# Self-attention of a PixArt block on one NeuronCore: another written order of a middle unit's steps

## The reference, cut to what matters

```python
def adaln(x, t, w, b):
    emb = t @ w + b
    scale, shift = jnp.split(emb, 2, axis=-1)
    return layernorm(x) * (1.0 + scale) + shift

def mha(xq, ctx, wq, wk, wv, wo, bo):
    q = (xq @ wq).reshape(b, sq, H, DH).transpose(0, 2, 1, 3)
    k = (ctx @ wk).reshape(b, sk, H, DH).transpose(0, 2, 1, 3)
    v = (ctx @ wv).reshape(b, sk, H, DH).transpose(0, 2, 1, 3)
    scores = jnp.einsum('bhqd,bhkd->bhqk', q, k) / math.sqrt(DH)
    attn = jax.nn.softmax(scores, axis=-1)
    out = jnp.einsum('bhqk,bhkd->bhqd', attn, v)
    return out.transpose(0, 2, 1, 3).reshape(b, sq, INNER) @ wo + bo

h1 = adaln(x, t, norm1_w, norm1_b)
x = mha(h1, h1, ...) + x          # self-attention, 1024 queries, 1024 keys
h2 = adaln(x, t, norm2_w, norm2_b)
x = mha(h2, context, ...) + x     # cross-attention, 77 keys
x = glu_ff(adaln(x, ...)) + x     # then a quantised feed-forward net
```

## Time and profile before

| | us |
|---|---|
| median of 3 runs | 1274.09 |
| lowest and highest run | 1270.73, 1281.41 |
| the profiled execution's own time | 1271.72 |
| its span in the trace | 1269.9 |
| PE busy in the span | 1130.8 |
| units 0 to 15 of self-attention, about | 61 to 815 |

### The profile page before, as it was taken

One profiled execution on the slowest core, in us unless ns is written; L12 is line 12 of the kernel. 1 busy time (PEld: TensorE's weight loads), 2 busy tenths in 40 slices (PEclk: granted clock), 3 DMA queues, 4 the chain that ended last, 5 costly groups with the idle time before them and its releaser, 6 DMA issues.

```text
span 1269.9 us, 30602 instructions
## 1 busy us (share of the span) xinstructions
PE 1130.8 (89%) x12732; PEld 736.7 (58%) x12739; DVE 867.5 (68%) x1724; ACT 593.1 (47%) x855; POOL 681.1 (54%) x602
## 2 busy tenths in 40 slices
PE   4789999999999999999999998988999799799776
PEld 1245655665665665655665665666666566365554
DVE  5667767756756667757757658578679666765764
ACT  3335454444344344444444455444445442465555
POOL 5657866755655666757755654356346443511230
PEclk7799999999999999999999999999999999999987
DMA  7230220220220220220220222234333520000001
GB/s 270 58 109 2 51 51 2 52 51 7 46 51 9 45 51 3 51 51 2 52 51 2 51 51 68 43 67 121 82 64 74 162 76 1 1 5 14 17 1 34
DMA packets 41855, 63.52 MB, mean 50 GB/s; under 512 B 11460, under 2 KB 22384, under 8 KB 41462
## 3 DMA queue, kind: packets, MB, share of 16 engines
q1 hardware_dynamic: 40413, 60.91, 19.1%
q10 hardware_dynamic: 1304, 0.66, 0.2%
HBM read 20.63 MB, written 2.10 MB: 18 GB/s over the span
## 4 chain that ended last, share of the span: by engine, by line
PE 61%; DVE 17%; DMA 7%; ACT 6%; issue 6%; SPq 2%; POOL 1%; ACTq 0%; DVEq 0%
PE outs L806 9%; PE scores L865 7%; PE scores L866 7%; PE mixed L827 6%; DMA head_operands<-neg_max_rows 5%; PE outs L783 4%; PE scores L924 4%; PE outs L890 3%; PE outs L888 3%; PE outs L889 3%; PE outs L940 3%; DVE maxes L1670 3%; DVE exps_rest L1693 2%; PE outs L816 2%; SPq L673 2%
## 5 line engine op out<-in xcount | busy, mean ns | idle before, releaser
L1459 POOL TENSOR_TENSOR exps_rest<-exps 128x1024 f16<-128x1024 f32 (+1 forms) x297 | 511.5, 1730 | 317.3 <-ACT exps L1169 316.5
L1169 ACT ACTIVATE exps<-scores 128x1024 f32<-128x1024 f32 (+1 forms) x320 | 296.8, 936 | 281.3 <-PE scores L866 251.7
L1670 DVE TENSOR_REDUCE maxes<-mixed 128x1 f32<-128x512 f32 x512 | 334.3, 684 | 81.1 <-PE mixed L827 77.6
L865 PE MATMUL scores<-head_operands 128*128 128x512 f16 (+1 forms) x576 | 219.8, 382 | 24.3 <-DMA head_operands<-neg_max_rows 23.7
L888 PE MATMUL outs<-values,exps 128*128 128x65 f16 (+1 forms) x2176 | 226.6, 193 | 1.2 <-POOL exps_rest L1459 1.2
L889 PE MATMUL outs<-values,exps 128*128 128x64 f16 (+1 forms) x2176 | 226.6, 192 | 0.0
L890 PE MATMUL outs<-values,exps_rest 128*128 128x65 f16 (+1 forms) x2176 | 226.4, 194 | 0.0
L866 PE MATMUL scores<-head_operands 128*128 128x512 f16 (+1 forms) x576 | 219.6, 381 | 0.0
L889 PEld LDWEIGHTS outs<-values,exps 128*128 128x128 bf16 (+1 forms) x2176 | 200.5, 98 | 24.8 <-issue 0.2
L888 PEld LDWEIGHTS outs<-values,exps 128*128 128x128 bf16 (+1 forms) x2176 | 201.6, 98 | 22.7 <-POOL exps_rest L1459 2.2
L890 PEld LDWEIGHTS outs<-values,exps_rest 128*128 128x128 f16 (+1 forms) x2176 | 200.4, 97 | 0.0
(11 more groups left out here) (200 smaller groups left out, 1599.7 us busy)
## 6 DMA issues: line engine op xcount, KB each, us to landing
head_operands<-qk_pairs SPq DMA_DIRECT2D x128, 256.0 KB, 4.2
head_operands<-qk_pairs SPq DMA_DIRECT2D x32, 128.0 KB, 2.4
stage<-in_L_xcond_ff_w_dram SPq DMA_DIRECT2D x3, 1024.0 KB, 5.6
residual<-in_x_dram SPq DMA_DIRECT2D x4, 512.0 KB, 9.7
stage<-in_L_ffn_w_dram SPq DMA_DIRECT2D x2, 1024.0 KB, 5.1
head_operands<-in_x_dram SPq DMA_DIRECT2D x1, 2048.0 KB, 10.2
out_dram<-out_tile SPq DMA_DIRECT2D x16, 128.0 KB, 1.7
attn_outT<-in_L_xcond_attn_wq_dram SPq DMA_DIRECT2D x1, 1024.0 KB, 8.2
```

Source lines behind the costliest of these rows:

```text
L865: mm(o, kb[:, KH, :], hb[:, QS, :], start=True, stop=False)
L1169: A(E[0:a.ks, c % RING, 0:n], SP_[c % 2][0:a.ks, 0:n], ACT.Exp, scale=SCALE).then_inc(s.exps, 1)
L1459: G.tensor_tensor(R[0:a.ks, c % RING, 0:n], e, e.bitcast(BF16).rearrange("p (n two) -> p n two", two=2)[:, :, 1], ALU.subtract).then_inc(s ...
L1670: V.tensor_reduce(mx[:, h, t, kh:kh + 1], m[:, :], AX_X, ALU.max).then_inc(s.maxed, 1)
```

## The change

Only the table `SELF_UNIT` and the lags change; no step is added or taken away. The old and the new order up to chunk 8, with the untouched steps left out:

```diff
 SELF_UNIT = (
-    ("scores", 1), ("rest", 0), ("max", 0, 1, 8), ("max", 0, 1, 9), ("q", 1, 0),
+    ("max", 0, 1, 8), ("scores", 1), ("rest", 0), ("max", 0, 1, 9), ("q", 1, 0),
...
-    ("slot", 1), ("slot", 2), ("slot", 3), ("values", 1), ("k", 1, 0), ("max", 0, 1, 12), ("scores", 4),
-    ("rest", 3), ("max", 0, 1, 13), ("k", 1, 1), ("values", 2), ("scores", 5), ("scores", 6), ("rest", 4),
-    ("rest", 5), ("max", 0, 1, 14), ("norm1", 0), ("max", 0, 1, 15), ("projB", 0), ("scores", 7), ("rest", 6),
-    ("values", 3), ("row", 0, 1), ("v", 1, 0), ("slot", 4), ("slot", 5), ("values", 4), ("values", 5),
-    ("max", 1, 0, 0), ("max", 1, 0, 1), ("normT1", 0), ("slot", 6), ("values", 6), ("scores", 8), ("rest", 7),
+    ("slot", 1), ("slot", 2), ("values", 1), ("k", 1, 0), ("scores", 4), ("scores", 5), ("k", 1, 1),
+    ("max", 0, 1, 12), ("rest", 3), ("max", 0, 1, 13), ("values", 2), ("rest", 4), ("rest", 5), ("scores", 6),
+    ("max", 0, 1, 14), ("norm1", 0), ("slot", 3), ("max", 0, 1, 15), ("projB", 0), ("rest", 6), ("values", 3),
+    ("row", 0, 1), ("rest", 7), ("v", 1, 0), ("slot", 4), ("scores", 7), ("slot", 5), ("values", 4),
+    ("normT1", 0), ("values", 5), ("max", 1, 0, 0), ("max", 1, 0, 1), ("values", 6), ("scores", 8),
...
-    ("scores", 12), ("slot", 10), ("rest", 11), ("max", 1, 0, 12), ("projA", 1), ("max", 1, 0, 13),
+    ("scores", 12), ("rest", 11), ("max", 1, 0, 12), ("max", 1, 0, 13),
+    ("slot", 10), ("projA", 1), ("lo1", 1), ("values", 10), ("norm", 1), ("max", 1, 0, 14), ("rest", 12),
...
-SELF_LAGS = {"POOL": {"proj": 5, "norm": -2},
-             "ACT": {"scores": -1, "row": 1},
-             "DVE": {"rest": -4}}
+SELF_LAGS = {"POOL": {"proj": 5, "norm1": 2, "lo": 1},
+             "ACT": {"scores": -1, "row": 1, "hi": 2, "q": -2},
+             "DVE": {"rest": -3, "v": -1, "k": 2}}
```

More of the change, by code:

```diff
@@ L63 @@
-    ("values", 3), ("row", 0, 1), ("v", 1, 0), ("slot", 4), ("slot", 5), ("values", 4), ("values", 5),
-    ("max", 1, 0, 0), ("max", 1, 0, 1), ("normT1", 0), ("slot", 6), ("values", 6), ("scores", 8), ("rest", 7),
-    ("max", 1, 0, 2), ("norm", 0), ("hi1", 0), ("max", 1, 0, 3), ("v", 1, 1), ("scores", 9), ("rest", 8),
-    ("max", 1, 0, 4), ("max", 1, 0, 5), ("values", 7), ("projA", 0), ("normT", 0), ("slot", 7),
-    ("max", 1, 0, 6), ("slot", 8), ("lo1", 0), ("norm1", 1), ("hi", 0), ("scores", 10), ("max", 1, 0, 7),
@@ L68 @@
-    ("values", 8), ("rest", 9), ("lo", 0), ("max", 1, 0, 8), ("scores", 11), ("rest", 10), ("max", 1, 0, 9),
-    ("hi1", 1), ("max", 1, 0, 10), ("projB", 1), ("slot", 9), ("values", 9), ("normT1", 1), ("max", 1, 0, 11),
-    ("scores", 12), ("slot", 10), ("rest", 11), ("max", 1, 0, 12), ("projA", 1), ("max", 1, 0, 13),
-    ("slot", 11), ("lo1", 1), ("values", 10), ("norm", 1), ("max", 1, 0, 14), ("rest", 12), ("values", 11),
-    ("normT", 1), ("scores", 13), ("hi", 1), ("slot", 12), ("max", 1, 0, 15), ("scores", 14), ("slot", 13),
@@ L73 @@
[L73 to L79 removed]
+    ("max", 0, 1, 8), ("scores", 1), ("rest", 0), ("max", 0, 1, 9), ("q", 1, 0), ("max", 0, 1, 10), ("slot", 0),
@@ new lines @@
+    ("normT1", 0), ("values", 5), ("max", 1, 0, 0), ("max", 1, 0, 1), ("values", 6), ("scores", 8),
+    ("max", 1, 0, 2), ("norm", 0), ("hi1", 0), ("slot", 6), ("max", 1, 0, 3), ("v", 1, 1), ("scores", 9),
+    ("rest", 8), ("max", 1, 0, 4), ("max", 1, 0, 5), ("values", 7), ("normT", 0), ("slot", 7), ("projA", 0),
+    ("max", 1, 0, 6), ("lo1", 0), ("slot", 8), ("rest", 9), ("norm1", 1), ("hi", 0), ("scores", 10),
+    ("max", 1, 0, 7), ("values", 8), ("rest", 10), ("lo", 0), ("max", 1, 0, 8), ("scores", 11),
@@ new lines @@
+    ("max", 1, 0, 9), ("hi1", 1), ("max", 1, 0, 10), ("projB", 1), ("slot", 9), ("values", 9),
+    ("max", 1, 0, 11), ("normT1", 1), ("scores", 12), ("rest", 11), ("max", 1, 0, 12), ("max", 1, 0, 13),
+    ("slot", 10), ("projA", 1), ("lo1", 1), ("values", 10), ("norm", 1), ("max", 1, 0, 14), ("rest", 12),
+    ("values", 11), ("normT", 1), ("hi", 1), ("slot", 11), ("slot", 12), ("scores", 13), ("max", 1, 0, 15),
+    ("scores", 14), ("slot", 13), ("rest", 13), ("max", 1, 1, 0), ("row", 1, 0), ("values", 12),
@@ new lines @@
+    ("max", 1, 1, 1), ("lo", 1), ("rest", 14), ("scores", 15), ("values", 13), ("rest", 15), ("max", 1, 1, 2),
+    ("max", 1, 1, 3), ("slot", 14), ("out", 0, 0), ("scores", 16), ("max", 1, 1, 4), ("values", 14),
+    ("max", 1, 1, 5), ("values", 15), ("max", 1, 1, 6), ("max", 1, 1, 7), ("slot", 15), ("out", 0, 1),
+    ("slot", 16))
+SELF_LAGS = {"POOL": {"proj": 5, "norm1": 2, "lo": 1},
+             "ACT": {"scores": -1, "row": 1, "hi": 2, "q": -2},
+             "DVE": {"rest": -3, "v": -1, "k": 2}}
```

7 lines of the change are left out of this document (1 added, 6 removed).

## The result

| | before | after |
|---|---|---|
| median of 4 runs each, same chip, us | 1272.76 | 1257.78 |
| lowest and highest | 1270.73, 1281.41 | 1256.14, 1259.88 |
| profiled execution: time, span | 1271.72, 1269.9 | 1259.88, 1258.1 |

The ratio of the runs, after to before, is 0.9866, with a 95% interval of 0.984 to 0.9891: faster by 1.3%, just over the 1% that a measurement of this kernel can tell. (The two medians alone give 0.988.) The forecast for the median was 1258.5. The profiled execution is the slowest of the four after the change.

What follows compares the result with a forecast made beforehand. PE, busy 89% of the span, bounds the kernel. Ten units 7.4, units 8 to 11 6.2 less 1.6, unit 0 2.1: 14.1 us off 1271.7 makes 1257.6; median forecast 1258.5, range 1254 to 1263, 57%.

Steps and rivals of the forecast that it cites:

- A unit without `projB`: Ten units, worked on unit 4's clock: chunk 8's scores start 0.82 us earlier in unit 4; 7.4 us over the ten.
- The price at the row: In units without `projB`, PE waits 0.84 us for `neg_max` before head 1's row, where it waited 0.11.
- Rival 1: Price at the row underestimated: a DVE chain 0.65 us later costs ten units 6.5, giving 1264 to 1265; 20%.
- The rest of the unit keeps its order ... I count nothing there: Units without `projB`, after chunk 8's scores: order kept but for steps nobody waits for, so no gain or loss.
- this margin grows by 0.2: Head 0's restacked operands before the next unit's first maximum: restack 0.33 us later, maximum at 274.53 instead of 273.98.
- the first account: Units 8 to 11, with `projB`: no price at the row; gains of 1.68, twice 1.3, and 1.95, together 6.2 us.
- I add 0.4 of waiting each: Units 8 to 11: row's transfer leaves just behind the fifth restack transfer and waits 0.4 us, 1.6 in all.
- the 4.0: Head 1's row transfer in the ten units without `projB`: assumed to take 4.0 us, leaving 0.2 us of room.
- rival 2: No change: row's transfer lands at a fixed distance from the restack, scores 0.33 us later in 14 units; 1274.2; 13%.
- Rival 3: Slower: ACT's queue gets its turn only behind all six restack transfers, row landing at about 277.9; 1285; 5%.
- the signs that the prediction named against itself: Transfers longer than 5 us, a wait at the row past 1.3, or a new wait before a `values`.
- a wait of 1.6 us may not do this: Unit 0, maximum 11: wait cut from 2.86 to 1.6 us may not halve PE's clock; 0.8 us taken for this.

Runs made afterwards that it cites:

- e8: The changed kernel with 32 more of PE's first small transposes (64 instructions) at its start; units 1 to 14 took 660.73 us, against 660.35 in the changed kernel.
- e5: The changed kernel with slot 11 again ahead of maximum 14; 1256.99 us in its one run.
- e9: e5 with 112 more of PE's first small transposes (224 instructions); median 1265.58 us, ratio 0.993 to the kernel before.
- e3: The kernel before, with `tokens8` ahead of DVE's part of `k` 0 in unit 0 alone; median 1270.3 us, ratio 0.9973.
- e6: e5 with head 1's maxima 12 to 15 one or two steps earlier; median 1256.18 us, ratio 0.9867 to the kernel before.
- e10: e6 with the next unit's first two maxima behind values 6; median 1254.94 us, ratio 0.9848 to the kernel before.
- e1: The kernel before, with only head 1's row and `v` 0 moved in front of chunk 7's scores; median 1261.56 us, ratio 0.99.
- e2: The kernel before, with only the keys' part of the new order, unit 0 unchanged; median 1267.88 us, ratio 0.9956.
- e4: The changed kernel with ACT's copy of head 1's row, and so its transfer's issue, behind chunk 7's exponential; 1289.65 us in one run.
- e7: The changed kernel measured once more, unedited; median 1259.67 us, ratio 0.9894 to the kernel before.

## Why the prediction was right, and where not

**A unit without `projB`.** Unit 4's account came out to the hundredth: 0.84 us in front of the row (0.83 measured), 0.10 in front of maximum 15, the gap of `k` 1 gone, PE ready 4.36 after the issue (4.32), period 46.6 (46.60). The price at the row was exact because each of the five DVE instructions had its row, and DVE stands still between none of them. Rival 1 (the price underestimated by 0.65) fell with this. Eight of the ten units lie within 0.4 of their forecast. The ten gave 5.3 us against 7.4.

The 2.1 that are missing come from two units: 6 (-0.38, not 0.82) and 14 (-1.16, not 0). The step that failed is "The rest of the unit keeps its order ... I count nothing there", with "this margin grows by 0.2" for the restacked operands. In unit 6 the margin was right and the transfer was not: a code packet that came at 6.3 us behind the restack's start before, and left its third transfer alone, comes at 5.2 now, as PE reaches the same instruction number at another place of the unit; e8 freed the unit and took 46.61. In unit 14 slot 11 isn't empty, as it is in all others; I had looked at it in the stage of a middle unit only. It cost 0.8 (e5). The late restack, which the prediction let stand for "this unit gives nothing", costs 1.1 in the new order (55.00 in e5 with it, 53.91 in e9 without), more than the 0.7 that the order gives this unit (54.63 before, 53.91 in e9). Before, the wait for it (1.07) stood in place of the one at chunk 8's scores, which was 0.07 there; now chunk 8's scores wait in no quiet unit, so that it comes on top. So 0.7 is won, 1.1 and 0.8 are lost, and -1.2 is left.

**The units 8 to 11.** 6.4 us measured; the 6.2 of the first account, not the 4.6 with the lengthening taken off. The term that fails is "I add 0.4 of waiting each": in the units 8, 10 and 11 the scores start 4.33 after the issue with no wait for the transfer, so it was no longer than that, and in unit 9 it was 4.5 and cost 0.3. By the last update of its semaphore it had landed after 3.7 in unit 10. There is luck in the 6.4, though: 1.0 of it is unit 10's long transfer before (4.75), which e3, with the same order in these units, didn't have (3.75). Against e3 the four units give 5.4.

**The transfer.** Issued 3.0 us behind the first restack transfer instead of 4.4, it let the scores go 4.32 after its issue in unit 4, and it wasn't what they waited for. The trace holds the updates of its semaphore, and the last of them tells the landing: 3.2 to 3.4 us after the issue in the quiet units, so that the 4.0 was too long and the room was 1 us and not 0.2. The same updates, read over all profiles, show the order that the durations hide. Counted from the unit's first restack transfer, the row lands in steps of about 1 us:

| row issued at, us | lands at, us, in most units | kernels and units |
|---|---|---|
| 2.2 to 3.0 | 6.0 to 6.5 | e6 and e10; the changed kernel, quiet units |
| 3.5 to 4.0 | 7.0 to 7.4 | the changed kernel's 8, 10, 11; e1; e2, quiet units |
| 4.4 | 8.3 to 8.5 | before, e3 |
| 5.2, 5.7, 6.1 | 9.3 to 9.5 | e2's 8, 9, 11; before's 8 and 11; e4 |

Nearly all exceptions land later, by 0.3 to 2.2 us, the units 3, 7 and 9 most often. So rival 2 (fixed distance from the restack) is refuted as it was put, by the profile after and by e4, but the landing does hang on the restack in part: within a step an earlier issue gains nothing, and over the edge of one it gains a whole us. The change crossed two such steps in a quiet unit (8.4 to 6.3) and two in the units 8 to 11 (9.3 to 7.2), and the 4.0 came out as enough with some luck. Why there are steps, no run shows. Rival 3 (ACT's queue behind all of the restack) is refuted by the profile after: in unit 4 the row lands 3.7 us ahead of the sixth restack transfer. Its own figure was short, by the way: that transfer lands 9.9 us behind the first one's issue in the kernel before, not 9.4.

Of the two statements quoted from the Trainium skill (DMA: Bandwidth & Descriptors, "Queues, rings and completion order"), the turns taken packet by packet fit: the small transfer lands in the midst of the large ones. The rule on the completion increment isn't decided here: the row of unit 4 lands 0.9 us ahead of the fourth restack transfer, which was issued before it, so its landing doesn't wait for whole earlier transfers, but how each DMA engine's writes are ordered the runs don't show.

**The signs.** Three of the signs that the prediction named against itself came up in single places, without its account of a quiet unit being wrong. The row's transfer took 5.2 us in unit 3, where the late restack hid it. A wait of 1.7 stands at head 0's row in unit 14 (e5 explains it). And a new wait of 0.5 stands in front of a `values` in unit 1, on POOL's `rest`, at 148.48 us; it isn't traced further.

**Unit 0.** 2.1 forecast, 0.9 in the profile after, 2.1 in the second one. The order gave more than 1.3: PE's wait at maximum 11 fell from 2.86 to 0.55, not to 1.6, since `tokens8` itself took 1.94 us and not 2.95. Of its four instructions three take 0.40 or 0.41 in either order, and one that starts while POOL's `rest` is running ends 0.15 us behind it: the fourth before (75.84, with `rest` from 75.60 to 77.67), the first after (71.87, with `rest` until 72.70). The new place meets the end of a `rest`, the old one nearly all of it. Durations of the four, in ns (least, median, longest), before and after:

```profile
L1569 DVE TENSOR_SCALAR residual<-residual,x_mean_var,x_rstd x4: 405/408/1982, 74.9 to 75.8; 128x256 f32<-128x256 f32 x4
...
L1570 DVE TENSOR_SCALAR residual<-residual,x_mean_var,x_rstd x4: 400/400/975, 71.9 to 73.4; 128x256 f32<-128x256 f32 x4
```

What the forecast had wrong is the clock: "a wait of 1.6 us may not do this" looked at one wait, and another one behind it, 2.0 us for the row's transfer at 87.69, can do the same. Whether the clock falls there isn't fixed by the program: it fell to half behind that wait in one profile and stayed at full in the next, and unit 0 was 1.25 us shorter there. e2, with the old order in unit 0, kept the full clock behind the same wait of 2.86 and took 61.52, only 0.25 less than before; against it, the new order at full clock (59.64) gave 1.9. Over all 13 profiles unit 0 took 61.5, 61.8 and 63.3 in the old order and 58.9 to 61.0 in the new one. So the order was the term to count, with about 2 and not 1.3, and the clock a thing of chance.

**The total.** The forecast sum without unit 0 was 12.0 (7.4 + 6.2 - 1.6) and 11.7 was measured; two errors of about 2 us, of opposite sign, hid each other. That is luck. The sum was made for the profiled execution, and there it said 1257.6 where 1259.88 was measured; the median came within 0.7 us of its forecast. The medians lie 15.0 apart, the two profiled spans 11.8: the difference is in the runs' own spread of some 4 us, in which the profiled execution after was the slowest.

## What to carry to other kernels

When a wait is moved ahead on an engine's list, price the step that becomes ready last in the new order by the chain of instructions that leads to it: where that engine is full and every link has a row, the price can come out exact, as it did here. Then go through each unit of the loop that carries something the others don't (a slot that is empty in all but one), since a stage-wise order moves these as well. This program fetches its own code on the DMA engines; where an exchange of data inside the core had less than 1 us of room, some units lost it to such a packet, and edits that changed when PE reached an instruction number dealt the losses out anew. A difference of 1 us in single iterations is then no verdict on the edit, and neither is one behind which the granted clock fell: look at it in each unit before a loss is explained (e2's unit 10, e3's unit 7).

## What the runs showed that was not expected

- A 16 KB code packet near the restack is 0.9 to 1.1 us long. Started 3.8 to 5.2 us behind a unit's first restack transfer, it made the third transfer 5.7 to 6.0 us long in every one of 28 units and cost 0.9 to 1.2 us where e8 freed a unit of it; 64 more instructions at PE's start moved the loss from the units 3, 6 and 14 to 2, 4 and 13 (e8).
- The same program keeps full clock behind waits of 0.8 and 2.0 us in one execution and drops to half behind them in another (the windows under e7). Where the clock fell in the middle units of the other runs, the unit was some 1.1 to 1.7 us longer than without it: e2's unit 10 and e3's unit 7 against before, e4's 3 and 7 against the loss of its unit 4.
- A DVE instruction on 128x256 fp32 that took 0.40 us alone, started while POOL subtracted 128x1024, ended 0.15 us behind POOL's instruction: it took 1.98 us in the old order of unit 0 and 0.97 in the new one.
- A 2 KB transfer beside the restack landed in steps of about 1 us counted from the restack's first transfer (6.3, 7.3, 8.4, 9.4), whatever its issue inside a step: issued at 2.2 or 3.0 it landed at 6.0 to 6.5, issued at 3.5 to 4.0 at 7.0 to 7.4.
